# The first round of three chunks written out ahead of each group's loop in an edge-count stage

## The reference

```
edge_index = stack([src, dst])
h = relu(layernorm(x))
q, k, v = h @ Wq + bq, h @ Wk + bk, h @ Wv + bv
adj = zeros((N, N)).at[edge_index[0], edge_index[1]].set(1.0)
a = (q @ k.T / sqrt(512)) * adj + (1 - adj) * -1e6
x = x + softmax(a) @ v
h = relu(layernorm(x))
# second layer: twice agg(h) = segment_sum(dinv[src] * dinv[dst] * h[dst], src), with loops added,
# around a batch norm, a relu and two 512x512 products
x = x + gcn(h)
```

## Time and profile before

| | us |
|---|---|
| median of 3 runs (310.0 to 310.64) | 310.06 |
| the profiled execution | 310.67 |
| its span | 308.9 |
| outside the span | 1.8 |

### The profile page before, as it was taken

One profiled execution on the slowest core, in us unless ns is written; L12 is line 12 of the kernel. 1 busy time (PEld: TensorE's weight loads), 2 busy tenths in 40 slices (PEclk: granted clock), 3 DMA queues, 4 the chain that ended last, 5 costly groups with the idle time before them and its releaser, 6 DMA issues.

```text
span 308.9 us, 4793 instructions
## 1 busy us (share of the span) xinstructions
PE 297.6 (96%) x1345; PEld 229.6 (74%) x1345; DVE 210.3 (68%) x471; ACT 143.8 (47%) x245; POOL 57.3 (19%) x95
## 2 busy tenths in 40 slices
PE   8998979899999999999999999999999999999995
PEld 7876436465665688888888888888788888878884
DVE  2878999999998748667657484767444388276311
ACT  3889943443455626635464445437622035243000
POOL 5254370000000260032121311203010044100000
PEclk9999999999999999999999999999999999999999
DMA  7707040000410216643643825133102000000221
GB/s 269 291 13 195 1 136 2 1 0 3 159 44 3 47 24 176 130 96 58 122 87 83 151 47 111 36 68 65 37 7 63 1 2 0 0 2 0 100 107 68
DMA packets 42311, 21.66 MB, mean 70 GB/s; under 512 B 35760, under 2 KB 36016, under 8 KB 42288
## 3 DMA queue, kind: packets, MB, share of 16 engines
q1 hardware_dynamic: 41744, 20.33, 26.4%
q10 hardware_dynamic: 544, 1.05, 0.9%
HBM read 10.88 MB, written 2.10 MB: 42 GB/s over the span
## 4 chain that ended last, share of the span: by engine, by line
PE 78%; DVE 8%; ACT 5%; issue 3%; DVEq 3%; DMA 1%; POOL 1%; ACTq 0%; POOLq 0%
PE ps L950 18%; PE ps L952 17%; PE ps L951 17%; PE ps L1200 9%; PE ps L1123 8%; PE ps L1016 6%; DVE src_oh L671 3%; PE ps L984 2%; DMA qk_raw<-L_gnn_Wk_in 1%; DVE dst_oh L673 1%; DVEq L671 1%; ACT T L428 1%; POOL lnc L351 1%; ACT T L423 1%; ACT WT L459 1%
## 5 line engine op out<-in xcount | busy, mean ns | idle before, releaser
L671 DVE TENSOR_SCALAR src_oh<-iota,ecol 128x512 f16 x149 | 44.5, 352 | 4.3 <-issue 3.2
L1016 PE MATMUL ps<-src_oh,dst_oh 128*128 x149 | 37.8, 382 | 5.2 <-DVE dst_oh L673 5.0
L1016 PEld LDWEIGHTS ps<-src_oh,dst_oh 128*128 x149 | 14.4, 104 | 25.4 <-issue 16.3
L1123 PE MATMUL ps<-cnt,qh 128*128 128x512 f32 x128 | 30.0, 391 | 0.3 <-ACT cnt L541 0.3
L1200 PE MATMUL ps<-qh,cnt 128*128 128x512 f32 x128 | 29.3, 390 | 0.0
L443 ACT ACTIVATE cnt<-ps 64x512 int16<-64x512 f32 x32 | 18.9, 592 | 20.7 <-PE ps L1030 20.3
L1123 PEld LDWEIGHTS ps<-cnt,qh 128*128 128x128 f32 x128 | 23.9, 188 | 5.6 <-DVE qh L829 0.7
L1200 PEld LDWEIGHTS ps<-qh,cnt 128*128 128x128 f32 x128 | 23.9, 188 | 5.3 <-DVE vb L931 0.3
L952 PE MATMUL ps<-v,pT 128*128 128x512 f32 x64 | 25.0, 390 | 0.0
L950 PE MATMUL ps<-hT,qh 128*128 128x512 f32 x64 | 24.9, 389 | 0.0
L950 PE MATMUL ps<-v,pT 128*128 128x512 f32 x64 | 24.9, 389 | 0.0
(11 more groups left out here) (178 smaller groups left out, 665.6 us busy)
## 6 DMA issues: line engine op xcount, KB each, us to landing
xt<-x_in SPq DMA_DIRECT2D x16, 256.0 KB, 3.2
out<-xt SPq DMA_DIRECT2D x8, 256.0 KB, 2.1
qk_raw<-L_gnn_Wk_in ACTq DMA_DIRECT2D x2, 512.0 KB, 4.7
qk_raw<-L_gnn_Wq_in SPq DMA_DIRECT2D x2, 512.0 KB, 6.6
wB_raw<-L_gnn_Wv_in SPq DMA_DIRECT2D x2, 512.0 KB, 8.8
wB_raw<-L_gnn_W_in SPq DMA_DIRECT2D x2, 512.0 KB, 3.7
w_raw<-L_gnn_W_in SPq DMA_DIRECT2D x2, 512.0 KB, 4.2
bias_row<-L_gnn_b_in SPq DMA_DIRECT2D x2, 256.0 KB, 3.8
```

The lines of the kernel that those rows point to most:

```text
L671: dve.tensor_scalar(src_oh[:, bass.ds(slot, 1), j, :].rearrange("p a n -> p (a n)"), iota[:, :], ecol[:, bass.ds(c + j, 1)], None, ALU.is_ ...
L1016: m = pe.matmul(ps[:, i % 2, :], dst_oh[:, bass.ds(slot, 1), :, j].rearrange("p a n -> p (a n)"), src_oh[:, bass.ds(slot, 1), j, :].rearra ...
L1123: m = pe.matmul(bank(g), qh[:, d, a, c * P:(c + 1) * P], cnt[:, d, n * HALF:(n + 1) * HALF], start=(d == 0 and a == 1), stop=last)
```

## The change

```
-PAD = 4
-ROUNDS = NW * (2 + NCH // UNROLL)
+PAD = 5
+ROUNDS = NW * (3 + NCH // UNROLL)
...
             chunks_of(i, first, LEAD)
-            with dve.Fori(first + LEAD, end, UNROLL) as c:
+            chunks_of(i, first + LEAD, UNROLL)
+            with dve.Fori(first + LEAD + UNROLL, end, UNROLL) as c:
                 chunks_of(i, c, UNROLL)
...
             chunks(i, LEAD, True)
-            with pe.Fori(first + LEAD, end, UNROLL):
+            chunks(i, UNROLL, False)
+            with pe.Fori(first + LEAD + UNROLL, end, UNROLL):
                 chunks(i, UNROLL, False)
```

## The result

The changed kernel takes 314.50 us (median of 4 runs, 314.12 to 316.05) against 310.03 us for the kernel before, measured beside it: a ratio of 1.0138, 95% interval 1.0111 to 1.0165. It is 4.5 us slower; 314.9 with a range from 313.2 to 316.6 was forecast. Its profiled execution took 314.49 us, with a span of 312.7.

The account below looks back on a forecast made before the run. PE, gapless from 103 us on, passes on any delay of the counts stage, where PE or DVE sets the pace by group. Terms 1.0 + 1.13 + 1.29 + 0.3 + 1.13 = 4.85 us on 310.06 gave 314.9 us, range 313.2 to 316.6.

Parts of the forecast that it names:

- The root: Loop entered with nothing left still runs once, so six groups of five chunks each gain a round of three chunks.
- Groups 11 and 16: PE already waits for DVE there, so the added round closes each group 1.13 us later.
- DVE's price: What one added three-chunk round takes on DVE: 1.13 us.
- Groups 13 and 14: DVE is 3.9 us ahead before group 14, so PE sets the pace: 2 x 0.645 = 1.29 us.
- PE's price: What one added three-chunk round takes on PE: 0.215 us a chunk, 0.645 us a round.
- Group 15: No added round, but DVE's lost lead makes the ring a brake: 0.3 us, bounds 0 and 0.75.
- Groups 1 and 2: Two added rounds, partly absorbed by DVE's idle time, make group 3 late by 1.0 us, bounds 0.80 and 1.34.
- The small edits: Fewer compare-branches, longer straight code and `PAD` pieces of 133 entries on POOL: all costed at nothing.
- DVE sets the pace everywhere: Rival: each of the four late rounds costs 1.13 us, with code and POOL on top: 317.1 us, chance 0.07.
- more is absorbed: Rival: groups 1 and 2 cost nothing and late rounds cost PE's price, 2.6 us: 312.7 us, chance 0.06.
- The empty loop: Rival: an empty loop is jumped over, no round is added and time stays 310.1 us, chance 0.03.
- the rival on the faster side: Empty loops jumped over, DVE's sequencer sets the pace in groups 3 to 16, 1.4 us given back: 308.7 us, chance 0.02.

Follow-up runs that it names:

- the guarded loop: The changed kernel with a test around the loop on both engines, so it is skipped where nothing is left: 309.87 us, ratio 0.9998.
- the six rounds in loops: The kernel before, loops kept and no straight code, with `end` raised by three chunks in groups 1, 2, 11, 13, 14, 16, `PAD` 8: 315.87 us, ratio 1.018.
- the memsets: Six added rounds in loops on the kernel before, plus ten tiny memsets ahead of DVE's first round to move its later code: 316.31 us, ratio 1.02.

## Why the prediction was right, point by point

**The root.** The loop tests at its bottom and runs once where nothing is left: shown by the 29 branches, and by the guarded loop, which takes the six rounds away and with them the whole cost.

**Groups 11 and 16** at DVE's price: 1.13 and 1.06 us in the change, 1.13 each where they stand alone. The wait that the prediction named for the last round, some 0.5 us, is 0.30. It did not enter the sum; it is what DVE's round (1.13) leaves over PE's three chunks (0.83), and should have been worked out so. The 0.51 of the earlier trace rows is the wait after a shorter run of two.

**Groups 13 and 14** at PE's price: 1.27 with group 12 against 1.29, and 0.65 and 0.66 where they stand alone. Runs of eight without a wait, as forecast.

**Group 15**: the mechanism was right and the size too small, 0.46 against 0.3, and 0.56 where groups 13 and 14 have the only added rounds. DVE's second round waits 0.46 us for the ring (100.03), and PE, which began the group at 100.93 and would be through five chunks at 100.93 + 5 x 0.215 = 102.0, gets the third round at 102.62: 0.62 us late. The step that was mis-sized put it at "some 0.4". Less the 0.16 us of before, 0.62 gives the 0.46.

**Groups 1 and 2**: 1.10 against 1.0, within the bounds given, and by the path told: DVE reaches the splitting of `Wv` 6.64 - 4.49 = 2.15 us later, where two rounds at 1.13 us were taken (2.26), its wait of 0.92 us for ACT is eaten whole, PE comes to the `v` product 1.22 us late, and the ring passes that on to group 3. But that the size came out is luck. With the loops kept, the same two rounds make DVE 7.29 - 4.49 = 2.80 us later and cost 2.01 at the end of group 3, over the upper bound of 1.34. The working has nothing for the longer one-hots beside POOL in group 2, which raise the price, and nothing for the stop of 0.43 us leaving its place ahead of group 2, which lowers it: the prediction named that stop and kept it at zero for the change, with one more as the upper end, and that it could go was seen only as part of a rival. Two misses with opposite signs lie in that term, 1.0 us for the rounds in loops and 0.8 to 0.9 for the straight code.

**Groups 4 to 10**: 0 was forecast, -0.25 measured; the guarded loop, which has the same straight rounds, shows about -0.1 there, and the second profile of the changed kernel -0.27. Nothing was run that separates these groups. That straight rounds give back a little there is likely, and not shown.

**The small edits.** Code, branches and `PAD` at nothing: the guarded loop, with the same `PAD`, the same straight rounds and the tests on top, comes out at 0.9998 [0.9987, 1.001], so their sum lies within about 0.4 us of zero. That does not make each of them nothing. POOL's last eight pieces of 133 entries take 5.73 us, 5.70 with 132, so the odd length does not double POOL's work; but three one-hots of DVE beside them take 1.07 to 1.10 us in the changed kernel, 1.03 with 132 and 1.04 or 1.05 with the 136 of the six rounds in loops. For the three or so rounds that it meets in group 3 that is 0.1 to 0.2 us, which the prediction put at nothing.

The stop of 0.43 us belongs to a place in the code, as moving it showed. That it is the crossing from one block of code to the next is argued, not shown, and the prediction's remark that the 0.43 us shows such a crossing goes further than its rows; the view behind the earlier trace rows also holds a packet on a second instruction queue, q8. For it speaks that one packet on q14 follows the pause wherever it lies: at 19.4 us behind the one that ends at 19.14 before, at 18.5 behind 17.87 in the changed kernel, at 18.3 behind 17.61 with the memsets. If it is, the sentence of the Trainium skill ("Runtime: NRT & Kernel Launch", Instruction fetch mechanics) that calls the cost of a crossing mostly hidden holds for the sum of this change and not for the place ahead of group 2. The same section of the Trainium skill says that kernels prefer full unrolling where possible, and gives as one reason that a taken branch can break the sequential fetch. Straight code is cheaper in groups 1 and 2 here (1.18 us against 2.01), by the stop that moved and by what DVE's rounds meet; that the branches themselves cost time no run here shows, and 16 more of them on each engine in the guarded loop leave the time as it was.

**Where the closing of group 16 falls.** Near 108 us was forecast and 106.98 seen. The difference is the start of the stage, 15.65 in place of 16.63 us; from the first one-hot on it is 91.33 us where 86.56 + 4.85 = 91.4 was forecast. The start of group 3 on DVE, 29.68 - 15.65 = 14.03 us after it, is 0.85 later than before (29.81 - 16.63 = 13.18), near the lower of the two bounds.

**The rivals.** That DVE sets the pace everywhere falls with the 0.65 us of groups 13 and 14. That more is absorbed falls with groups 1, 2, 11 and 16. The empty loop is not jumped over; where it is made to be, the time is that of before and not less, so the 1.4 us of the rival on the faster side are not there, unless the added tests take them up, which at 50 ns each on DVE's sequencer (16 x 0.05 = 0.8 us) they could do in part at most. The 0.43 us that this rival took as the largest stop for issue was not the largest: the earlier trace rows has 0.75 and the earlier trace rows 0.54. Nothing else rests on it.

## What to carry to other kernels

A loop that tests at its bottom runs once even where nothing is left, so each round peeled off ahead of it adds a round wherever the trip count becomes zero: read the trip counts from the trace (branches against bodies) before peeling. A test around the loop took the whole cost away here and cost nothing that the times can tell. Price an added round by the engine that is waited for in that very group, and look one group further, where the lost lead of the other engine comes due. Count by stage from the stage's own first instruction, as two executions of one kernel can be a microsecond apart before it begins.

## What the runs showed of the hardware that was not expected

The start of the stage is not the same from execution to execution: 16.63 and 15.47 us for one kernel in two profiles, and the closings of all sixteen groups are moved with it, by 1.14 to 1.16 us. Runs of that kernel on one chip lie between 309.35 and 311.07 us, which is a scatter of the same size. A difference of under a microsecond between two single profiles of this kernel says nothing until that is taken off.

DVE stops for 0.4 us at a place that belongs to the code: ahead of group 2 before, not there in the changed kernel (a pause of about 0.15 us lies in group 1 instead), and inside the loop of group 1 when ten instructions were put ahead of it. A loop over such a place paid at each pass, 0.34 and 0.27 us.

16-bit one-hots on DVE (three of 128x512) take 0.88 us alone and 1.01 to 1.10 us beside POOL's pieces of 16-bit targets, where 133 entries in a piece go with the upper end. POOL is held up by DVE as well, though not in these rows by one-hots: in the second execution of the kernel before, a POOL operation of two columns, 0.20 us elsewhere, took 2.47 us from 19.91 on, the time in which DVE splits `Wv` (19.96 to 22.31). Its row in the timeline of POOL:

```profile
19.91 2.47 POOL L351 TENSOR_TENSOR lnc<-lnc 128x2 f32<-128x2 f32 x1
```
